# Expert layers with a stationary weight slot instead of turned inner rows

## The chip, the cores and the metric

The kernel runs on one core of a Trainium2 chip. The metric is device time in microseconds (us) of one execution. The engines are TensorE (PE, with its weight loads as PEld), VectorE (DVE), ScalarE (ACT), GpSimd (POOL) and SyncE (SP, which issues most DMAs). They run on their own and meet at semaphores.

## The reference, cut to what matters

A network of four blocks on 2 x 1024 tokens of width 128, all in fp32: a delta-rule attention, a mixture of experts (called f0), a softmax attention, and a second mixture of experts (f1). The change is in f0 and f1.

```
# f0: the two best of 8 experts for each token, hidden width F = 512
h = silu(x @ gate_w[e].T) * (x @ up_w[e].T)       # [tokens, 512]
y = h @ down_w[e].T                               # [tokens, 128]
out += y * gate_of_token
# f1: the best of 8 experts for each token, one down product for all
inter = gelu(x @ W1[e] + b1[e])                   # [tokens, 512]
y = inter @ Wo + bo + x                           # then a layer norm
```

## The kernel before

Tokens are sorted by expert. A tile is 128 rows that share one expert: at most 4096/128 + 7 = 39 tiles in f0 and 2048/128 + 7 = 23 in f1 (`tiles_of`). The layers are written out tile by tile, without a run-time loop; the expert of a tile is known only at run time, so an engine that needs that expert's weights first reads its number from SBUF into a register (`expert_of`, L338) and addresses the weights by the register.

Four functions give the four engines their lists: `experts_pe`, `experts_dve`, `experts_act`, `experts_pool`. In each, a step `s` handles several tiles at different stages (`Lag`): tile s, s-1, s-2, and so on. Nothing reorders the lists. For one tile the stages before are:

- POOL gathers the tile's 128 rows from DRAM into one of 4 slots of `e_x` (L470).
- PE turns them (`turn_x`, L367); DVE copies the turned rows to `e_xt` (L411).
- PE computes the inner product with `e_xt` as stationary operand and the expert's 512 weight columns moving: one matmul of 512 columns (L374), in f0 a second one for the other factor (L394). The result has tokens on partitions.
- f0: ACT takes silu of the first (L448), DVE multiplies by the second (L432). f1: DVE adds the bias of the expert (L418), a tile of [128, 8, 512] which a DMA has repeated over the partitions; ACT takes gelu (L451).
- PE turns the inner rows, four blocks of 128x128 (L389); ACT copies them to `e_ht` (L454). The down product needs the hidden dimension on partitions.
- PE multiplies by the down weights, four matmuls of 128 columns that add up (L383); DVE copies the 128x128 result to `e_y` (L426, below called the y copy); POOL scatters it to DRAM (L475).

An fp32 matmul stands in the trace as two passes, so one inner product is 2 rows, a down product 8, and the four turns of L389 are 4. In f1 DVE also carries four pairs of 128x512 additions (L436) at steps 8, 11, 14 and 17. Ahead of each layer a routing stage on DVE builds the tables; the SP queue meanwhile loads the weights (L639 in f1) and writes the normed rows to DRAM (L564), from which POOL gathers.

Of the kernel before, what the change touches and what calls it, by code (L numbers as in the profile page):

```python
# [11 lines left out]
P = 128  # L12
B, L, D = 2, 1024, 128
# [340 lines left out]
def experts_pe(c, name, top, gated):  # L354
    pe, ps, m, S = c.pe, c.psum, c.mem, c.sem
    n, ident, wup, wdown = tiles_of(top), m["ident"], m["e_up"], m["e_down"]
    xs, xt, h, ht = m["e_x"], m["e_xt"], m["e_h"], m["e_ht"]
    landed = [S(f"{name}_landed{k}") for k in range(SLOTS)]
    turned, copied, up, again = (S(f"{name}_{w}") for w in ("turned", "copied", "up", "again"))
    hidden = S(name + ("_hidden" if gated else "_acted"))  # L360
    hturned, hcopied, down, ready = (S(f"{name}_{w}") for w in ("hturned", "hcopied", "down", "ready"))
    pe.wait_ge(S(name + "_owned"), 1)
    pe.wait_ge(S(name + "_weights"), c.weights)

    def turn_x(a):
        pe.wait_ge(landed[a.slot], 16 * (a.turn + 1))
        pe.transpose(ps[:, 6, 0:P], xs[:, a.slot, :], ident[:]).then_inc(turned, 1)  # L367

    for s in range(n + 3):
        x0, u, g, d = (Lag(s, lag, n) for lag in range(4))  # L370
        if u.there:
            e = expert_of(c, pe, u.t)
            pe.wait_ge(copied, u.t + 1)
            pe.matmul(ps[:, u.pair, :], xt[:, u.pair, :], merged(wup[:, bass.ds(e, 1), 0:F]), start=True, stop=True).then_inc(up, 1)  # L374
        if not gated and x0.there:
            turn_x(x0)
        if d.there:
            ed = bass.ds(expert_of(c, pe, d.t), 1) if gated else slice(0, 1)
            if d.t >= 2:
                pe.wait_ge(ready, d.t - 1)  # L380
            pe.wait_ge(hcopied, d.t + 1)
            for f in range(FC):
                mm = pe.matmul(ps[:, 5 + 2 * d.pair, 0:P], ht[:, f * P:(f + 1) * P], merged(wdown[:, ed, f * P:(f + 1) * P]),  # L383
                               start=f == 0, stop=f == FC - 1)
            mm.then_inc(down, 1)
        if g.there:
            pe.wait_ge(hidden, g.t + 1)
            for f in range(FC):
                mm = pe.transpose(ps[:, 4, f * P:(f + 1) * P], h[:, g.pair, f * P:(f + 1) * P], ident[:])  # L389
            mm.then_inc(hturned, 1)  # L390
        if gated and x0.there:
            turn_x(x0)
        if gated and u.there:
            pe.matmul(ps[:, 2 + u.pair, :], xt[:, u.pair, :], merged(wup[:, bass.ds(e, 1), F:2 * F]),  # L394
                      start=True, stop=True).then_inc(again, 1)
# [5 lines left out]
def experts_dve(c, name, top, gated, x=None):  # L401
# [3 lines left out]
    turned, copied, up, again, acted = (S(f"{name}_{w}") for w in ("turned", "copied", "up", "again", "acted"))  # L405
# [3 lines left out]
    def turn_x(a):  # L409
        dve.wait_ge(turned, a.t + 1)  # L410
        dve.tensor_copy(xt[:, a.pair, :], ps[:, 6, 0:P]).then_inc(copied, 1)  # L411

    for s in range(n + 3):
        x0, u, g, d = (Lag(s, lag, n) for lag in range(4))
        if not gated and u.there:
            e = expert_of(c, dve, u.t)
            dve.wait_ge(up, u.t + 1)
            dve.tensor_tensor(sg[:, u.pair, :], ps[:, u.pair, :], merged(m["e_bias"][:, bass.ds(e, 1), :]), ALU.add).then_inc(hidden, 1)  # L418
        if not gated and x0.there:
            turn_x(x0)  # L420
        if d.there:
# [3 lines left out]
            yp = ps[:, 5 + 2 * d.pair, 0:P]  # L425
            dve.tensor_copy(y[:, d.slot, :], yp).then_inc(ready, 1)  # L426
        if gated and x0.there:
            turn_x(x0)
        if gated and u.there:
            dve.wait_ge(again, u.t + 1)  # L430
            dve.wait_ge(acted, u.t + 1)
            dve.tensor_tensor(h[:, u.pair, :], sg[:, u.pair, :], ps[:, 2 + u.pair, :], ALU.mult).then_inc(hidden, 1)  # L432
# [6 lines left out]
def experts_act(c, name, top, gated):  # L439
    act, ps, m, S = c.act, c.psum, c.mem, c.sem  # L440
    n, sg, h, ht = tiles_of(top), m["e_sg"], m["e_h"], m["e_ht"]
    up, acted, hidden, hturned, hcopied = (S(f"{name}_{w}") for w in ("up", "acted", "hidden", "hturned", "hcopied"))
    act.wait_ge(S(name + "_owned"), 1)
    for s in range(n + 2):
        u, g = Lag(s, 1, n), Lag(s, 2, n)
# [6 lines left out]
        if g.there:  # L452
            act.wait_ge(hturned, g.t + 1)
            act.copy(ht[:], ps[:, 4, :]).then_inc(hcopied, 1)  # L454


def experts_pool(c, name, top, src, dst):
# [21 lines left out]
    for s in range(n + 3):  # L479
        x0, d = Lag(s, 0, n), Lag(s, 3, n)  # L480
# [41 lines left out]
def sorted_memory(c, w, top, up):  # L522
# [3 lines left out]
    for name, shape in (("lo", [P, NT, NE]), ("wide", [P, NT, 32]), ("eq", [P, NT, NE]), ("best", [P, NT]),  # L526
# [6 lines left out]
                        ("e_sg", [P, 2, F]), ("e_h", [P, 2, F]), ("e_ht", [P, F]), ("e_y", [P, SLOTS, D]),  # L533
# [93 lines left out]
def ffn1_memory(c, w):  # L627
# [5 lines left out]
    c.sb("e_bias", [P, NE, F])  # L633


def ffn1_sp(c, w, x, out):
    for name in ("up", "down", "bias"):
        source = w["f1_" + name]
        c.sp.dma_start(c.mem["e_" + name][:], source.partition_broadcast(P) if name == "bias" else source).then_inc(c.sem("f1_weights"), 16)  # L639
# [126 lines left out]
def ffn1_layout(a, out):  # L766
    out["f1_rw"] = np.pad(a["L1_ffn_Wr"].T, ((0, 0), (0, 32 - NE)))
    out["f1_up"] = a["L1_ffn_W1"].transpose(1, 0, 2)
    out["f1_bias"] = a["L1_ffn_b1"]
# [1815 lines left out]
```

## Time and profile before

| | us |
|---|---|
| median of 3 runs | 923.98 (923.12 to 925.49) |
| the profiled execution | 930.92 |
| its span in the profile | 929.6 |
| f0's expert tiles, first turn to the last y copy | 274.7 to 403.2 |
| f1's expert tiles, first turn to the last y copy | 835.7 to 907.6 |

Busy shares over the span: PE 81%, DVE 72%, ACT 55%, POOL 26%. These are means over stages with different limits; the two expert stages are 200 us of the 930 and are read by themselves below. Times in the rows are from the span's start. A row of the timeline merges like instructions that follow each other.

### The profile page before, as it was taken

Reading aid. Unit: us, or ns where it says so; the run is one execution under the profiler, and the core shown is the slowest. Engines: PE = TensorE matmul, PEld = TensorE weight load, DVE = VectorE, ACT = ScalarE, POOL = GpSimd, SP = SyncE. Lnnn points to the kernel's source line nnn. Section 1 sums busy time; section 2 is a strip of 40 time slices with the busy share of each in tenths; the row PEclk is TensorE's granted clock in tenths of the full one; section 3 lists DMA queues with packets and bytes.
Section 4 is the critical chain, followed back from the end, with each engine's and each line's share of the span. In section 5 each row is a group of like instructions: output and inputs, shape, how many; then the busy total and the mean of one; then the engine's idle time right before and its main releaser. Section 6 shows DMA issues by size and latency. Waiting matters only on the chain. (4 is left out here: it accounts for less than half of the span.)

```text
span 929.6 us, 17693 instructions
## 1 busy us (share of the span) xinstructions
PE 756.1 (81%) x6703; PEld 325.6 (35%) x6704; DVE 667.4 (72%) x1316; ACT 511.1 (55%) x1012; POOL 243.9 (26%) x297
## 2 busy tenths in 40 slices
PE   6999978967329999927887999999999999728880
PEld 2343256633216766714111222222222222215660
DVE  7868964477763344338786999999999998753545
ACT  4744413646203333344346888888888889704343
POOL 0130010323055666460651200000010000025653
PEclk9999979988659999977658999999999999958996
DMA  3520010000731111131876030312300000061113
GB/s 94 119 65 2 1 25 5 4 1 0 269 129 38 43 43 43 35 102 52 233 159 194 2 81 2 81 26 58 80 3 2 3 2 12 1 252 44 43 35 96
DMA packets 40618, 57.62 MB, mean 62 GB/s; under 512 B 12424, under 2 KB 27920, under 8 KB 39768
## 3 DMA queue, kind: packets, MB, share of 16 engines
q1 hardware_dynamic: 36568, 48.36, 19.1%
q0 software_dynamic: 3968, 8.13, 3.1%
q8 instruction: 55, 0.90, 0.4%
q14 instruction: 27, 0.22, 0.1%
HBM read 37.54 MB, written 14.75 MB: 56 GB/s over the span
## 5 line engine op out<-in xcount | busy, mean ns | idle before, releaser
L1019 DVE TENSOR_REDUCE arena<-psum 128x1 f32<-128x1024 f32 x256 | 301.0, 1217 | 23.5 <-PE psum L903 20.7
L1158 ACT ACTIVATE arena<-psum 128x512 f32<-128x512 f32 x512 | 265.9, 605 | 53.7 <-PE psum L922 53.6
L903 PE MATMUL psum<-arena 56*128 56x512 bf16 x512 | 181.0, 413 | 10.7 <-DVE arena L1019 9.1
L922 PE MATMUL psum<-arena 59*128 59x512 bf16 x512 | 156.3, 390 | 5.1 <-ACT arena L1158 3.7
L933 PE MATMUL psum<-arena 128*32 128x512 f32 x1024 | 138.4, 612 | 8.7 <-issue 8.7
L922 PEld LDWEIGHTS psum<-arena 59*128 59x128 bf16 x512 | 38.4, 94 | 165.8 <-ACT arena L1158 142.1
L475 POOL DMA_INDIRECT rows_y<-arena x62 | 61.9, 998 | 61.3 <-DVE arena L426 57.9
L383 PEld LDWEIGHTS psum<-arena 128*128 128x128 f32 x496 | 62.4, 191 | 37.9 <-issue 29.5
L383 PE MATMUL psum<-arena 128*128 (+1 forms) x496 | 66.9, 278 | 9.1 <-ACT arena L454 6.0
L374 PE MATMUL psum<-arena 128*128 x124 | 67.2, 625 | 3.5 <-DVE arena L411 2.7
L1227 POOL TENSOR_SCALAR arena<-arena 128x16 f32<-128x16 f32 x16 | 4.1, 254 | 249.5 <-DVE arena L1019 249.4
L470 POOL DMA_INDIRECT arena<-rows_x,arena x62 | 60.1, 969 | 35.4 <-issue 16.1
L903 PEld LDWEIGHTS psum<-arena 56*128 56x128 bf16 x512 | 37.5, 95 | 71.2 <-DVE arena L1019 69.0
L426 DVE COPY arena<-psum 128x128 f32<-128x128 f32 x62 | 18.1, 291 | 58.2 <-issue 36.3
L454 ACT COPY arena<-psum 128x512 f32<-128x512 f32 x62 | 36.2, 584 | 41.3 <-PE psum L389 37.9
L448 ACT ACTIVATE arena<-psum 128x512 f32<-128x512 f32 x39 | 23.3, 597 | 46.9 <-PE psum L374 46.9
L432 DVE TENSOR_TENSOR arena<-arena,psum 128x512 f32<-128x512 f32 x39 | 26.8, 688 | 23.5 <-PE psum L394 22.0
L2242 PE MATMUL psum<-arena 128*32 128x512 f32 x352 | 41.2, 593 | 0.2 <-DMA arena<-arena 0.2
L394 PE MATMUL psum<-arena 128*128 x78 | 40.8, 606 | 0.0
L389 PE MATMUL psum<-ident,arena 128*128 128x128 f32 x248 | 37.7, 275 | 0.0
L933 PEld LDWEIGHTS psum<-arena 128*32 128x32 f32 x1024 | 20.7, 108 | 42.4 <-issue 38.0
L418 DVE TENSOR_TENSOR arena<-psum,arena 128x512 f32<-128x512 f32 x23 | 15.9, 691 | 25.4 <-PE psum L374 19.5
(319 smaller groups left out, 1110.1 us busy)
## 6 DMA issues: line engine op xcount, KB each, us to landing
arena<-scr_k SPq DMA_DIRECT2D x15, 448.0 KB
arena<-scr_q SPq DMA_DIRECT2D x15, 448.0 KB
arena<-in_f_up SPq DMA_DIRECT2D x1, 4096.0 KB
arena<-rows_y SPq DMA_DIRECT2D x12, 256.0 KB, 4.5
scr_q<-arena SPq DMA_DIRECT2D x6, 384.0 KB, 3.7
arena<-in_f_down SPq DMA_DIRECT2D x1, 2048.0 KB
rows_x<-xn SPq DMA_DIRECT2D x2, 1024.0 KB, 16.8
arena<-in_f_up SPq DMA_DIRECT2D x1, 2048.0 KB, 8.4
```

Source lines behind the costliest of these rows:

```text
L374: pe.matmul(ps[:, u.pair, :], xt[:, u.pair, :], merged(wup[:, bass.ds(e, 1), 0:F]), start=True, stop=True).then_inc(up, 1)
L383: mm = pe.matmul(ps[:, 5 + 2 * d.pair, 0:P], ht[:, f * P:(f + 1) * P], merged(wdown[:, ed, f * P:(f + 1) * P]), start=f == 0, stop=f == FC ...
L389: mm = pe.transpose(ps[:, 4, f * P:(f + 1) * P], h[:, g.pair, f * P:(f + 1) * P], ident[:])
L394: pe.matmul(ps[:, 2 + u.pair, :], xt[:, u.pair, :], merged(wup[:, bass.ds(e, 1), F:2 * F]), start=True, stop=True).then_inc(again, 1)
L470: pool.indirect_dma_start(xs[:, t % SLOTS, :], None, src, index).then_inc(landed[t % SLOTS], 16)
L475: pool.indirect_dma_start(dst, index, y[:, d.slot, :], None).then_inc(stored[d.slot], 16)
L903: mm = pe.matmul(ps[:, bank + half, :], q[rows, k, h, (qh * 4 + qt) * P:(qh * 4 + qt + 1) * P], kk[rows, k, h, half * BLK:(half + 1) * BLK ...
L922: pe.matmul(ps[:, score_bank(n), :], kk[0:KA, k, h, kb * P:(kb + 1) * P], q[0:KA, k, h, qh * BLK:(qh + 1) * BLK], start=True, stop=True).t ...
L933: mm = pe.matmul(ps[32 * h:32 * h + 32, 7, :], va[:, kb, (st % NG) * HG + h, :], pt[:, (u % 3) * HG + h, :], start=kb == 0, stop=kb == NTB ...
L1019: dve.tensor_reduce(mx[:, qh, h * 4 + qt:h * 4 + qt + 1], ps[:, bank:bank + 2, :].rearrange("p a b -> p (a b)"), X, ALU.max).then_inc(S("a ...
L1158: act.activation(pt[:, (u % 3) * HG + h, :], ps[:, score_bank(n), :], ACT.Exp, scale=float(HD) ** -0.5).then_inc(S("a1_exp"), 1)
L2242: mm = pe.matmul(ps[32 * h:32 * h + 32, fir_bank(n, i), :], m["a0_wfir"][:, (g0 + g) * H0 + h, :], v4[:, h, b, PAD + t0 - 4 * g:PAD + t0 - ...
```

## The change

The two operands of the inner product change places. The weights become the stationary operand, 128 hidden columns at a time, and the turned tokens `e_xt` the moving one. The result then has the hidden dimension on partitions, as the down product needs it, so `e_ht`, L389 and L454 go. A stationary operand addressed by a register is not used; instead DVE copies the expert's first 512 weight columns to one of two slots `e_w` (new L412), and in f0 ACT copies the other 512 (new L448). Both need the expert's number, so DVE in f0 and ACT in f0 read it now, and DVE in f1 reads it twice. PE reads it once a tile in f0 (for the down weights) and never in f1. The bias of f1 is now one value for each partition and block, [128, 8, 4], loaded by a small DMA and repeated along the free dimension in the addition (new L420). A tile passes through one step fewer: n + 2 steps in place of n + 3.

```
-    for s in range(n + 3):                                            # PE
-        if u.there: e = expert_of(...); wait copied
-            pe.matmul(ps[:, u.pair, :], xt[:, u.pair, :], merged(wup[:, bass.ds(e, 1), 0:F]), ...)
+    def inner(a, half, bank, done):
+        for f in range(FC):
+            at = slice(half * F + f * P, half * F + (f + 1) * P)
+            mm = pe.matmul(ps[:, bank, f * P:(f + 1) * P], w[:, a.pair, at], xt[:, a.pair, :], start=True, stop=True)
+        mm.then_inc(done, 1)
+    for s in range(n + 2):
+        x0, u, d = (Lag(s, lag, n) for lag in range(3))
+        if u.there:
+            pe.wait_ge(copied, u.t + 1)
+            pe.wait_ge(picked, u.t + 1)
+            inner(u, 0, u.pair, up)
+            if gated:
+                pe.wait_ge(picked2, u.t + 1)
+                inner(u, 1, 2 + u.pair, again)
+        if x0.there:   # wait landed, turn the tile's rows
...
-        if g.there:    # wait hidden
-            for f in range(FC):
-                mm = pe.transpose(ps[:, 4, f * P:(f + 1) * P], h[:, g.pair, f * P:(f + 1) * P], ident[:])
...
+        if x0.there:                                                   # DVE
+            e = expert_of(c, dve, x0.t)
+            if x0.t >= 2:
+                dve.wait_ge(up, x0.t - 1)
+            dve.tensor_copy(m["e_w"][:, x0.pair, 0:F], merged(m["e_up"][:, bass.ds(e, 1), 0:F])).then_inc(picked, 1)
+        if u.there and gated:
+            dve.wait_ge(again, u.t + 1)
+            dve.wait_ge(acted, u.t + 1)
+            dve.tensor_tensor(h[:, u.pair, :], sg[:, u.pair, :], ps[:, 2 + u.pair, :], ALU.mult).then_inc(hidden, 1)
...
+        if x0.there and gated:                                         # ACT
+            e = expert_of(c, act, x0.t)
+            if x0.t >= 2:
+                act.wait_ge(again, x0.t - 1)
+            act.copy(m["e_w"][:, x0.pair, F:2 * F], merged(m["e_up"][:, bass.ds(e, 1), F:2 * F])).then_inc(picked2, 1)
...
-        if g.there:
-            act.wait_ge(hturned, g.t + 1)
-            act.copy(ht[:], ps[:, 4, :]).then_inc(hcopied, 1)
...
-    c.sb("e_bias", [P, NE, F])
+    c.sb("e_bias", [P, NE, FC])
```

PE's list in f0 for one tile, before (L338 reads the expert's number, an ISA row forms an address, L374 and L394 are the inner products, L383 the down product, L389 the turns of the inner rows, L367 the turn of the tokens):

```order
L374 ISA [waits f0_copied]
L374 MATMUL psum<-arena 128x512
L338 TENSOR_LOAD arena
L338 ISA x2
L383 ISA [waits f0_hcopied,f0_ready]
L383 MATMUL psum<-arena 128x128
L389 MATMUL psum<-ident,arena 128x128 [waits f0_hidden]
L389 MATMUL psum<-ident,arena 128x128 x3
L367 MATMUL psum<-ident,arena 128x128 [waits f0_landed0]
L394 ISA
L394 MATMUL psum<-arena 128x512
```

and after (L370 is the inner product, its first four for one factor, the next four for the other; L384 the turn of the tokens, L391 the down product):

```order
L370 MATMUL psum<-arena 128x128 [waits f0_picked,f0_copied]
L370 MATMUL psum<-arena 128x128 x3
L370 MATMUL psum<-arena 128x128 [waits f0_picked2]
L370 MATMUL psum<-arena 128x128 x3
L384 MATMUL psum<-ident,arena 128x128 [waits f0_landed0]
L338 TENSOR_LOAD arena
L338 ISA x2
L391 ISA [waits f0_hidden,f0_ready]
L391 MATMUL psum<-arena 128x128
```

The second inner product has moved from behind the turn of the next tile to ahead of it, and both inner products now stand together in front of the turn and the down product.

DVE's list in f0 for two tiles, before (L411 copies the turned tokens, L432 multiplies, L426 is the y copy):

```order
L411 COPY arena<-psum 128x128 [waits f0_turned]
L432 TENSOR_TENSOR arena<-arena,psum 128x512 [waits f0_acted,f0_again]
L426 COPY arena<-psum 128x128 [waits f0_down]
L411 COPY arena<-psum 128x128 [waits f0_turned]
L432 TENSOR_TENSOR arena<-arena,psum 128x512 [waits f0_acted,f0_again]
```

and for one tile and a half after (L412 copies the weights to the slot, L416 multiplies, L424 copies the turned tokens, L429 is the y copy):

```order
L338 TENSOR_LOAD arena
L338 ISA x2
L412 ISA [waits f0_up]
L412 COPY arena<-arena 128x512
L416 TENSOR_TENSOR arena<-arena,psum 128x512 [waits f0_acted,f0_again]
L424 COPY arena<-psum 128x128 [waits f0_turned]
L429 COPY arena<-psum 128x128 [waits f0_down]
L338 TENSOR_LOAD arena
```

The copy of the turned tokens has moved from ahead of the multiplication to behind it.

DVE's list in f1 after, for one tile (L420 adds the bias):

```order
L338 TENSOR_LOAD arena
L338 ISA x2
L412 ISA [waits a0_firm]
L412 COPY arena<-arena 128x512
L338 TENSOR_LOAD arena
L338 ISA x2
L420 ISA [waits a0_firm]
L420 TENSOR_TENSOR arena<-psum,arena 128x512
```

The names of the waits are left over from an earlier use of the same semaphores (here it is `f1_up`). Where one number was read for a tile, two are read now, one ahead of the weight copy and one ahead of the addition.

## Rows read from the trace of the kernel before

**Rows 1.** The page: busy us, share of the span and instructions of each engine.

```profile
PE 756.1 (81%) x6703; PEld 325.6 (35%) x6704; DVE 667.4 (72%) x1316; ACT 511.1 (55%) x1012; POOL 243.9 (26%) x297
```

**Rows 2.** Window in f0: length, busy (count) PE, PEld, DVE, ACT, POOL, clock, DMA.

```profile
300.00:390.00 90.00, 90.00 (x484) 61.78 (x482) 36.39 (x87) 33.69 (x57) 54.74 (x56) 1.00 0.15 42
```

**Rows 3.** Timeline in f0: start, us, engine, line, operation, count, idle before.

```profile
288.46 1.02 PE L374 MATMUL psum<-arena 128*128 x2
288.66 0.69 DVE L432 TENSOR_TENSOR arena<-arena,psum 128x512 f32<-128x512 f32 x1 [0.57 <-PE psum L394]
289.32 1.05 PE L383 MATMUL psum<-arena 128*128 x8
290.21 0.60 PE L389 MATMUL psum<-ident,arena 128*128 128x128 f32 x4
```

**Rows 4.** Timeline: a weight load that waited, once in f0, once in f1.

```profile
279.94 0.69 DVE L432 TENSOR_TENSOR arena<-arena,psum 128x512 f32<-128x512 f32 x1 [1.53 <-issue]
280.68 0.42 PEld L389 LDWEIGHTS psum<-ident,arena 128*128 128x128 f32 x4 [0.86 <-DVE arena L432]
...
868.10 0.97 PEld L383 LDWEIGHTS psum<-arena 128*128 128x128 f32 x8 [1.69 <-issue]
869.10 0.60 PE L389 MATMUL psum<-ident,arena 128*128 128x128 f32 x4
```

**Rows 5.** Timeline of one f1 tile.

```profile
871.25 0.69 DVE L418 TENSOR_TENSOR arena<-psum,arena 128x512 f32<-128x512 f32 x1
871.86 0.28 DVE L411 COPY arena<-psum 128x128 f32<-128x128 f32 x1
872.20 0.29 DVE L426 COPY arena<-psum 128x128 f32<-128x128 f32 x1
873.25 0.27 PE L367 MATMUL psum<-ident,arena 128*128 128x128 f32 x1
873.57 0.69 DVE L418 TENSOR_TENSOR arena<-psum,arena 128x512 f32<-128x512 f32 x1 [1.08 <-PE psum L374]
```

**Rows 6.** Line L338, DVE's queue, 872 to 873.3: ns min/median/max, first and last start.

```profile
L338 DVEq SEQ_ASSERT  x1: 23/23/23, 872.8 to 872.8; - x1
```

**Rows 7.** Groups by shape on DVE: busy us, mean ns, idle before.

```profile
L1636 DVE TENSOR_SCALAR arena<-arena 128x512 f32<-128x512 f32 x8 | 3.5, 483 | 3.3 <-ACT arena L1902 3.3
```

**Rows 8.** POOL in f1: line L475 (as rows 6), then rows of the timeline.

```profile
L475 POOL DMA_INDIRECT rows_y<-arena x23: 967/987/1401, 846.2 to 907.9; - x23
...
861.15 0.69 DVE L436 TENSOR_TENSOR x<-x,arena 128x512 f32<-128x512 f32 x1
861.29 1.40 POOL L475 DMA_INDIRECT rows_y<-arena  x1 [0.30 <-issue]
865.57 0.97 POOL L470 DMA_INDIRECT arena<-rows_x,arena  x1 [0.30 <-issue]
870.35 1.13 POOL L475 DMA_INDIRECT rows_y<-arena  x1 [0.30 <-DVE arena L426]
```

**Rows 9.** Timeline: last inner products of both layers, f0's last y copy, f1's first.

```profile
398.09 1.02 PE L394 MATMUL psum<-arena 128*128 x2
402.91 0.29 DVE L426 COPY arena<-psum 128x128 f32<-128x128 f32 x1 [2.22 <-PE psum L383]
...
836.69 2.07 PE L374 MATMUL psum<-arena 128*128 x2 [0.58 <-DVE arena L411]
...
900.49 1.02 PE L374 MATMUL psum<-arena 128*128 x2
```

**Rows 10.** Timeline: the last table of the routing and the first gather, f0 and f1.

```profile
270.79 0.20 DVE L312 SCALAR_TENSOR_TENSOR arena<-arena 128x40 int32<-128x40 f32 x1
...
271.87 1.19 POOL L470 DMA_INDIRECT arena<-rows_x,arena  x1 [6.50 <-DVE arena L312]
...
831.90 0.18 DVE L312 SCALAR_TENSOR_TENSOR arena<-arena 128x24 int32<-128x24 f32 x1
...
832.88 1.05 POOL L470 DMA_INDIRECT arena<-rows_x,arena  x1 [3.56 <-DMA rows_x<-xn]
```

More of the change, by code:

```diff
@@ L355, in experts_pe @@
     pe, ps, m, S = c.pe, c.psum, c.mem, c.sem
-    n, ident, wup, wdown = tiles_of(top), m["ident"], m["e_up"], m["e_down"]
-    xs, xt, h, ht = m["e_x"], m["e_xt"], m["e_h"], m["e_ht"]
+    n, ident, wdown, w = tiles_of(top), m["ident"], m["e_down"], m["e_w"]
+    xs, xt, h = m["e_x"], m["e_xt"], m["e_h"]
     landed = [S(f"{name}_landed{k}") for k in range(SLOTS)]
-    turned, copied, up, again = (S(f"{name}_{w}") for w in ("turned", "copied", "up", "again"))
+    turned, copied, up, again, picked, picked2 = (S(f"{name}_{w}") for w in ("turned", "copied", "up", "again", "picked", "picked2"))
     hidden = S(name + ("_hidden" if gated else "_acted"))
-    hturned, hcopied, down, ready = (S(f"{name}_{w}") for w in ("hturned", "hcopied", "down", "ready"))
+    down, ready = S(name + "_down"), S(name + "_ready")
     pe.wait_ge(S(name + "_owned"), 1)
     pe.wait_ge(S(name + "_weights"), c.weights)
-    def turn_x(a):
-        pe.wait_ge(landed[a.slot], 16 * (a.turn + 1))
-        pe.transpose(ps[:, 6, 0:P], xs[:, a.slot, :], ident[:]).then_inc(turned, 1)
-    for s in range(n + 3):
-        x0, u, g, d = (Lag(s, lag, n) for lag in range(4))
+    def inner(a, half, bank, done):
[5 more added lines that the diff above has]
+        x0, u, d = (Lag(s, lag, n) for lag in range(3))
         if u.there:
-            e = expert_of(c, pe, u.t)
             pe.wait_ge(copied, u.t + 1)
-            pe.matmul(ps[:, u.pair, :], xt[:, u.pair, :], merged(wup[:, bass.ds(e, 1), 0:F]), start=True, stop=True).then_inc(up, 1)
-        if not gated and x0.there:
-            turn_x(x0)
+            pe.wait_ge(picked, u.t + 1)
[4 more added lines that the diff above has]
+        if x0.there:
+            pe.wait_ge(landed[x0.slot], 16 * (x0.turn + 1))
+            pe.transpose(ps[:, 6, 0:P], xs[:, x0.slot, :], ident[:]).then_inc(turned, 1)
         if d.there:
@@ L380, in experts_pe @@
                 pe.wait_ge(ready, d.t - 1)
[L381 removed]
+            pe.wait_ge(hidden, d.t + 1)
             for f in range(FC):
[L383 removed]
+                mm = pe.matmul(ps[:, 5 + 2 * d.pair, 0:P], h[:, d.pair, f * P:(f + 1) * P], merged(wdown[:, ed, f * P:(f + 1) * P]),
                                start=f == 0, stop=f == FC - 1)
             mm.then_inc(down, 1)
[L386 to L395 removed]
 BIAS_STEPS = {8: 0, 11: 1, 14: 2, 17: 3}
@@ L424, in experts_dve @@
             dve.wait_ge(down, d.t + 1)
[L425 to L432, printed above, removed]
+            dve.tensor_copy(y[:, d.slot, :], ps[:, 5 + 2 * d.pair, 0:P]).then_inc(ready, 1)
         if not gated and s in BIAS_STEPS:
@@ L478, in experts_pool @@
         gather(t)
-    for s in range(n + 3):
-        x0, d = Lag(s, 0, n), Lag(s, 3, n)
+    for s in range(n + 2):
+        x0, d = Lag(s, 0, n), Lag(s, 2, n)
         if top == 1 and x0.there and x0.more:
@@ L638, in ffn1_sp @@
         source = w["f1_" + name]
[L639 removed]
+        c.sp.dma_start(c.mem["e_" + name][:], source).then_inc(c.sem("f1_weights"), 16)
     c.weights = 48
```

34 lines of the change are left out of this document (17 added, 17 removed).

## The prediction, made before the changed kernel ran

> **What bounds the kernel now.** I read the page first: PE is busy 81% of the span [rows 1], but that is a mean over stages, so I went to the windows of the two expert stages. In f0 PE is busy in all 90 of 90 us at full clock, with 484 matmul rows [rows 2]. A tile has 17 of them (1 turn of tokens, 4 for the two inner products, 8 for the down product, 4 turns of inner rows), so 28.5 tiles pass and one takes 3.16 us. The timeline splits it, by starts: an inner product 0.86 (288.46 to 289.32), the down product 0.89 (289.32 to 290.21) [rows 3]. What is left of 3.16, 0.55, is five turns of 0.11. f0 is bound by PE alone: the product that feeds the next step always waits in its queue.
>
> In f1 the sum of the same parts is 0.86 + 0.89 + 5 x 0.11 = 2.30 us, and two additions of the bias stand 2.32 apart in an undisturbed stretch [rows 5]. The whole stage is slower: from the end of the first inner product (836.69 + 2.07 = 838.7) to that of the last (900.49 + 0.86 = 901.35) [rows 9] lie 62.6 us for 22 tiles, 11.6 more than 22 x 2.32 = 51.0. The difference sits in single pauses of 1 to 2 us, as the 1.69 and 1.16 ahead of a down product with "issue" as their cause [rows 4]. I can't name what makes them. I take them as alike in both kernels; that they are not is a rival.
>
> POOL comes next in f1: a gather of 0.97, a scatter of 0.99 and 0.30 of idle ahead of each [rows 8] are 2.56 us a tile, more than PE's 2.32. It holds up nothing only because gathers run four tiles ahead.
>
> **f0, tile by tile.** PE loses four turns (0.44) and pays 2 x 0.89 in place of 2 x 0.86, since eight passes of 128 columns with a new weight each have the shape of the down product. PE's floor is 3 x 0.89 + 0.11 = 2.78 us. I don't take it, because of the order on DVE: the copy of the turned tokens now stands behind the multiplication, which waits for the second inner product, and the next tile's first inner product waits for that copy. This is a closed loop, and it is longer than the floor. From the start of the turn, when the second product has just left PE:
> - to the start of the multiplication 0.20 (288.46 to 288.66) [rows 3];
> - from it to a copy behind it 0.61 (871.25 to 871.86), and the copy 0.28 [rows 5];
> - from the end of a DVE result to PE's weight load 0.05 (279.94 + 0.69 to 280.68) [rows 4];
> - a load that nothing covers: 868.10 to 869.10 is 1.00 where 0.89 is usual, so 0.11 [rows 4];
> - both inner products 1.78.
>
> The sum is 3.03. Meanwhile PE does the turn and the down product (1.00) and idles 0.25. Against 3.16 that is 0.13 x 38 = 4.9 us saved. The bounds: were the wait 0.18 and not 0.05 nothing is saved; at the floor it is 0.38 x 38 = 14.4. I stay with 3.03, as each link has its row.
>
> What was added beside it hides. DVE's weight copy is bounded by 0.48 (a one-input operation of this size [rows 7]) and 0.69 (a two-input one [rows 5]); with a register read (from the copy's start at 872.20 to 872.82, 0.62 [rows 5, 6], and an estimated 0.14 for the address) it ends, behind a y copy that starts 1.2 after the turn, by 1.2 + 0.76 + 0.69 = 2.65, and the multiplication behind it is due at 3.03 + 0.20. ACT trades a copy out of PSUM for one out of SBUF; it is busy 33.69 of 90 us [rows 2]. Without that cover a copy would cost up to 0.69 a tile, 27 us.
>
> A weight load is where a rule of the skill speaks against the change. The down product has the same shape as the new inner product: eight loads and eight passes in 0.89 us, 0.11 a pair [rows 3], so the loads lie behind the passes. The Trainium skill (TensorE: Matmul & The Clock Gate, Part 3, The mechanism) says that a load overlaps matmuls in flight only when its row group differs, and here each load fills all 128 rows. By that rule each load would be laid bare; the trace disagrees.
>
> **f0, the end.** From the end of the last second product (398.09 + 0.86 = 398.95) to the end of the last y copy (402.91 + 0.29) are 4.25 us [rows 9], over multiplication, turns, ACT's copy and down product. After: 0.20 + 0.69 + 0.05 + 0.11 + 0.89 + 0.20 + 0.29 = 2.43. That saves 1.8. f0: -6.7.
>
> **f1.** Two loops run beside each other. Through PE: 0.32 from the turn's start to the addition (873.25 to 873.57 [rows 5]; its address costs more than in f0), 0.61, 0.28, 0.05, 0.11, 0.89, sum 2.26. Through DVE alone: y copy, read of the number and address 0.76, weight copy, a second read 0.76 (issued as soon as the weight copy is), addition, 0.61 to the tokens' copy, and 0.20 to the y copy (0.34 where it waits [rows 5]): 2.33. So the pace stays at 2.32 and PE's four turns bring nothing. The four pairs of additions L436 (0.60 from one start to the next) hold DVE 1.2 each, of which the register reads cover all but some 0.35: +1.4. The end, from the last product to the end of the last scatter, is 907.9 + 0.97 - 901.35 = 7.5 us now [rows 8, 9]; after, 0.32 + 0.69 + 0.05 + 0.70 for gelu (an estimate, by the addition) + 0.05 + 0.11 + 0.89 + 0.20 + 0.29 + 0.28 + 0.97 = 4.55, so -3.0. By PE and DVE, f1 gains 1.6.
>
> POOL takes part of it. The slowest scatter, 1.40 in place of 0.99, ran beside an addition with two SBUF inputs on DVE, and the one of 1.13 likewise [rows 8]: beside such work POOL loses 0.14 to 0.41. The weight copy now runs every tile and POOL has no idle time to lose. Without pauses, f1 now ends at 838.7 + 51.0 + 7.5 = 897.2, and after, by PE, at 895.6. POOL has 38 operations left when it starts its first scatter (15 gathers, 23 scatters), 38 x 1.28 = 48.6; it starts some 1.8 earlier than 846.2 [rows 8], so it ends at 893.0 + 20 x (0.14 to 0.41) = 895.8 to 901.2. I take 0.18, by the smaller of the two stretched rows: 896.6, so f1 gains 0.6, with bounds of -1.6 and +4.0.
>
> The Trainium skill (GPSIMD Engine Reference, section 8, Key points) says that POOL shares its SBUF interfaces with VectorE and that two-port modes and two SBUF inputs contend. The stretched rows agree for two inputs; no row shows the copy's own mode.
>
> The bias now moves 16 KB and not 2 MB, and the first gather of f1 is shown as waiting for the rows' DMA [rows 10]. That looks like a gain and is none: the last table was ready at 832.08, and f0's gather, which waited for that table alone, began 0.88 after it (270.99 to 271.87), which here gives 832.96, where the gather began at 832.88. Bounds 0 and -0.5; I take 0.
>
> **Sum.** -6.7 - 0.6 = -7.3 us. The profiled execution took 930.92 (span 929.6), so 923.6 in a profile. The median of the runs is 6.9 below the profiled one; with the same distance the forecast is 923.98 - 7.3 = 916.7.
>
> **Rivals.**
> - No gain in f0's loop. Its links are single readings, and 0.13 more (a wait of 0.18) brings it to 3.16. Only the ends and f1 are left: -1.8 - 0.6 = -2.4, 921.6. For it: the margin is 4% of a tile. Against: each link is a row. 19%.
> - POOL binds f1. At 0.41 a tile f1 loses 4.0: -6.7 + 4.0 = -2.7, 921.3. In f0 POOL would need 2.56 + 0.41 = 2.97, still under 3.03. 12%.
> - DVE binds f1, the slower side. If a register read begins only when DVE has finished what is ahead of it, y copy 0.29 + 0.76 + 0.48 + 0.76 + 0.61 + 0.20 = 3.10 a tile: +0.78 x 22 = 17.2, with the end -3.0 and f0 -6.7 it is +7.5, 931.5. It decides from a pace of 2.32 + 9.7 / 22 = 2.76. Against: the reads finish 0.62 after the y copy's start while that copy lasts 0.29 [rows 5, 6], and one cannot tell from this pair whether the read waited. 17%.
> - The pauses in f1 go away. PE's list gets shorter and loses its register reads there: -7.3 - 11.6, 905.1. For it: they have no named cause and f0 has none. Against: the same. 9%.
> - The weight loads are laid bare: 0.19 more for each of 8 passes, 101 products, +150 us. 1%.
>
> The forecast itself has 42%, with a range of 912 to 921. Faster or slower is told from no change at 0.3%, 2.8 us, so at 921.2. The forecast, the fourth rival and half of the first two fall on the faster side, together 0.66, rounded to 0.65; the other half is no change, with a little of the slower rival at a lower price: 0.17; slower 0.18. The range of 907 to 927 leaves out the far ends of the third and fourth.
>
> **What would show it.** In f0, PE with a gap of about 0.25 us ahead of each first inner product, released by DVE's copy of the tokens, and a pace of 3.03; a pace of 2.8 or 3.2 proves the loop wrong. From f0's last second product to the last y copy 2.4. In f1, a pace near 2.3 between pauses, POOL without idle time, scatters of 1.1 to 1.4; a pace of 3.1 with DVE idle behind register reads is the slower rival. The first gather of f1 still about 0.9 behind L312. The forecast falls if the pauses differ in number.

## The result, and the profile after

The changed kernel takes 916.13 us (median, 914.98 to 918.17, four runs), the kernel before 923.55 (921.95 to 925.49, four runs): ratio 0.9929, interval 0.9908 to 0.995, which is 7.4 us faster (4.6 to 8.5 by the interval). The forecast was 916.7. The profiled executions differ by more, 929.6 to 916.8 in span, and most of this part is about where those 12.8 us and the 7.4 agree and where they don't. One result ahead of all: on another chip the same change made the kernel 6.6 us slower, by pauses of a kind that the trace of before shows in f1.

f0 first, the timeline of the changed kernel (start, duration, engine, line, operation, shapes, idle time before it and what released it). One tile runs from L416 to L416:

```profile
288.09 0.14 PEld L384 LDWEIGHTS psum<-ident,arena 128*128 128x128 f32 x1
288.20 0.27 PE L384 MATMUL psum<-ident,arena 128*128 128x128 f32 x1
...
288.31 1.06 PE L391 MATMUL psum<-arena 128*128 x8
288.40 0.69 DVE L416 TENSOR_TENSOR arena<-arena,psum 128x512 f32<-128x512 f32 x1 [0.84 <-PE psum L370]
...
289.01 0.28 DVE L424 COPY arena<-psum 128x128 f32<-128x128 f32 x1
289.34 1.86 PEld L370 LDWEIGHTS psum<-arena 128*128 128x128 f32 x16 [0.17 <-DVE arena L424]
...
290.17 0.43 DVE L412 COPY arena<-arena 128x512 f32 x1 [0.48 <-issue]
...
291.12 0.14 PEld L384 LDWEIGHTS psum<-ident,arena 128*128 128x128 f32 x1
291.23 0.27 PE L384 MATMUL psum<-ident,arena 128*128 128x128 f32 x1
...
291.43 0.69 DVE L416 TENSOR_TENSOR arena<-arena,psum 128x512 f32<-128x512 f32 x1 [0.83 <-PE psum L370]
```

These lines answer to [rows 3]. Read them as a ring: the turn's pass starts at 288.20, the multiplication 0.20 later, the copy of the tokens 0.61 after that, it ends at 289.29, PE's load follows 0.05 later at 289.34, and the next turn's pass stands at 291.23, 1.89 on: 3.03 in all. The only idle time in PE's records is the 0.17 that L370's load waits for L424; against the floor of 2.78 the wait costs 0.25.

The windows (busy time and number of instructions per engine, granted clock, DMA share, GB/s) show why the busy share would have misled:

```profile
300.00:390.00 90.00, 90.00 (x744) 84.91 (x743) 47.77 (x119) 36.12 (x60) 56.80 (x59) 1.00 0.16 45
845.00:885.00 40.00, 35.47 (x281) 32.26 (x279) 30.04 (x73) 10.07 (x16) 30.86 (x31) 1.00 0.18 50
```

PE reads 90.00 of 90, as before [rows 2], though it waits in every tile: the modelled ends of the passes cover a gap of 0.2 us. What tells is the number of loads, 743 in place of 482.

f1 is bound by VectorE in more than half of its tiles now, and by PE in the others. POOL's lines show that it isn't POOL:

```profile
857.60 0.68 DVE L420 TENSOR_TENSOR arena<-psum,arena 128x512 f32<-128x512 f32 x1
...
858.40 0.27 DVE L429 COPY arena<-psum 128x128 f32<-128x128 f32 x1
...
859.84 0.69 DVE L420 TENSOR_TENSOR arena<-psum,arena 128x512 f32<-128x512 f32 x1 [0.54 <-PE psum L370]
...
860.45 0.28 DVE L424 COPY arena<-psum 128x128 f32<-128x128 f32 x1
...
860.79 0.29 DVE L429 COPY arena<-psum 128x128 f32<-128x128 f32 x1
861.41 0.97 POOL L470 DMA_INDIRECT arena<-rows_x,arena  x1 [0.30 <-issue]
861.57 0.43 DVE L412 COPY arena<-arena 128x512 f32 x1 [0.48 <-issue]
...
862.33 0.69 DVE L420 TENSOR_TENSOR arena<-psum,arena 128x512 f32<-128x512 f32 x1 [0.34 <-PE psum L370]
...
863.34 0.68 DVE L433 TENSOR_TENSOR xn<-xn,arena 128x512 f32<-128x512 f32 x1
863.94 0.68 DVE L433 TENSOR_TENSOR x<-x,arena 128x512 f32<-128x512 f32 x1
863.97 1.49 POOL L470 DMA_INDIRECT arena<-rows_x,arena  x1 [0.30 <-issue]
```

From L420 at 859.84 to L420 at 862.33 are 2.49 us, all of it VectorE's own list: 0.61 to the tokens' copy, 0.34 to y, 0.78 to the weight copy, 0.76 to the next addition. The 0.48 ahead of L412, put down to "issue", is the read of the tile's expert number. The interval ahead of it (857.60 to 859.84) is 2.24, the loop through PE. The 22 intervals of the stage have a mean of 2.52 (836.11 to 891.55). The first two are 3.18 and 3.53, and PE's granted clock was 0.50 there, 1.2 GHz:

```profile
836.00:842.00 6.00, 5.11 (x24) 4.95 (x24) 2.61 (x7) 2.54 (x3) 2.60 (x4) 0.50 0.13 37
```

The other 20 have a mean of 2.44: eight lie at 2.24 to 2.33, where the addition starts 0.32 to 0.39 behind PE's turn, as with an idle VectorE, and twelve at 2.42 to 2.73, where it starts 0.49 to 0.79 behind, held by VectorE's own list. The gather beside the weight copy (861.41) takes 0.97 as ever, the one beside the two-input additions 1.49.

The ends, from the same timeline, answer to [rows 9]:

```profile
397.60 0.69 DVE L416 TENSOR_TENSOR arena<-arena,psum 128x512 f32<-128x512 f32 x1 [1.67 <-PE psum L370]
...
398.54 0.97 PEld L391 LDWEIGHTS psum<-arena 128*128 128x128 f32 x8 [0.28 <-issue]
...
399.81 0.29 DVE L429 COPY arena<-psum 128x128 f32<-128x128 f32 x1 [0.96 <-PE psum L391]
...
891.55 0.69 DVE L420 TENSOR_TENSOR arena<-psum,arena 128x512 f32<-128x512 f32 x1 [1.17 <-PE psum L370]
...
894.85 0.96 POOL L475 DMA_INDIRECT rows_y<-arena  x1 [0.93 <-DVE arena L429]
```

From first turn to last y copy f0 takes 122.4 us where it took 128.5: 6.1 less. From first turn to the end of the last scatter f1 takes 62.8 where it took 73.2, 10.4 less; the stretches ahead of f0, between the layers and behind f1, which the change doesn't touch, are 3.8 longer in sum. The 10.4 hold the pauses of 1 to 2 us that the profiled f1 of before had. Its time, 930.92, is none of the four timed ones and lies 5.4 above the slowest of them, while every other profiled execution here is among its kernel's timed runs or, for the repeat of the kernel before, within the range of those beside it. So the timed runs of before had fewer pauses than the profiled one, or that one ran on another chip; on which it ran isn't on record.

### The profile page after: what moved, and what is told of

Read it like the earlier page. It is cut to its first block and busy times, and to the rows that moved or that the text cites. A ratio compares the mean times of both kernels' runs of the same rounds, so it can differ in the third digit from the quotient of the medians.

```text
span 916.8 us, 18626 instructions
## 1 busy us (share of the span) xinstructions
PE 747.2 (82%) x7061; PEld 364.4 (40%) x7062; DVE 689.2 (75%) x1378; ACT 499.5 (54%) x989; POOL 245.0 (27%) x297
## 5 line engine op out<-in xcount | busy, mean ns | idle before, releaser
L370 PE MATMUL psum<-arena 128*128 128x128 f32 x808 | 110.9, 290 | 7.9 <-DVE arena L424 7.2
L370 PEld LDWEIGHTS psum<-arena 128*128 128x128 f32 x808 | 99.0, 198 | 19.4 <-DVE arena L424 19.4
L475 POOL DMA_INDIRECT rows_y<-arena x62 | 62.1, 1001 | 47.7 <-DVE arena L429 43.1
L470 POOL DMA_INDIRECT arena<-rows_x,arena x62 | 60.9, 982 | 31.6 <-issue 16.8
L391 PE MATMUL psum<-arena 128*128 (+1 forms) x496 | 66.5, 278 | 0.9 <-ACT arena L454 0.8
L391 PEld LDWEIGHTS psum<-arena 128*128 128x128 f32 x496 | 61.1, 194 | 1.2 <-DVE arena L429 0.9
L451 ACT ACTIVATE arena<-psum 128x512 f32<-128x512 f32 x39 | 23.3, 597 | 59.6 <-PE psum L370 59.6
L416 DVE TENSOR_TENSOR arena<-arena,psum 128x512 f32<-128x512 f32 x39 | 26.8, 686 | 33.4 <-PE psum L370 33.4
L412 DVE COPY arena<-arena 128x512 f32 x62 | 27.3, 440 | 26.6 <-issue 26.1
L448 ACT COPY arena<-arena 128x512 f32 x39 | 24.1, 619 | 34.8 <-DVE arena L303 19.5
L454 ACT ACTIVATE arena<-arena 128x512 f32<-128x512 f32 x23 | 14.5, 630 | 40.2 <-DVE arena L420 40.2
L1982 ACT ACTIVATE arena<-psum 128x64 f32<-128x64 f32 x32 | 7.2, 224 | 41.8 <-PE psum L2264 41.7
```

The lines of the kernel that those rows point to most:

```text
L370: mm = pe.matmul(ps[:, bank, f * P:(f + 1) * P], w[:, a.pair, at], xt[:, a.pair, :], start=True, stop=True)
L391: mm = pe.matmul(ps[:, 5 + 2 * d.pair, 0:P], h[:, d.pair, f * P:(f + 1) * P], merged(wdown[:, ed, f * P:(f + 1) * P]), start=f == 0, stop= ...
L412: dve.tensor_copy(m["e_w"][:, x0.pair, 0:F], merged(m["e_up"][:, bass.ds(e, 1), 0:F])).then_inc(picked, 1)
L470: pool.indirect_dma_start(xs[:, t % SLOTS, :], None, src, index).then_inc(landed[t % SLOTS], 16)
L475: pool.indirect_dma_start(dst, index, y[:, d.slot, :], None).then_inc(stored[d.slot], 16)
```

## The experiments

Twelve runs were made, on four chips, here called A to D; each chip was used for one stretch of time only, so what is put down to a chip below could also belong to the moment. Whether the chip of the forecast is one of them isn't on record. The kernel before was timed on each beside them. "Interval" is the time from one DVE operation behind the inner product (L416 or its like in f0, L420 in f1) to the next; a pause is an interval more than 0.7 above the median. In f1 the median itself varies (2.25 to 2.79), and most counts take in one or both of the first two intervals (3.2 to 3.6 us, the slow start). On chip B these are all that is counted, but for one of 3.34 in the version with both edits. Of pauses past the start, the kernels on chips A and C have four to six in f1.

| kernel | chip | us | before | ratio | f0 interval, pauses | f1 interval, pauses |
|---|---|---|---|---|---|---|
| f0 only | A | 944.82 | 934.86 | 1.010 | 3.47, 11 | 2.89, 7 |
| f1 only | A | 932.31 | 934.86 | 0.996 | 3.14, 0 | 2.91, 5 |
| before | A | 936.66 | 934.86 | (one run) | 3.14, 0 | 2.96, 7 |
| one more load | A | 939.51 | 934.86 | 1.0055 | 3.41, 10 | 2.90, 6 |
| changed | B | 914.98 | 922.00 | 0.992 | 3.03, 0 | 2.55, 1 |
| early copy in f0 | B | 904.69 | 922.00 | 0.980 | 2.77, 0 | 2.53, 1 |
| f1's copy on ACT | B | 912.65 | 922.00 | 0.989 | 3.03, 0 | 2.40, 2 |
| both | B | 900.19 | 922.00 | 0.975 | 2.77, 0 | 2.31, 1 |
| f0 only | C | 941.61 | 932.93 | 1.009 | 3.40, 9 | 2.99, 4 |
| changed | C | 939.55 | 932.93 | 1.007 | 3.43, 10 | 2.94, 5 |
| double copy in f0 | C | 937.66 | 932.93 | 1.0045 | 3.41, 10 | 2.93, 6 |
| both | D | 901.20 | 922.45 | 0.978 | 2.77, 0 | 2.30, 0 |

**One half at a time, chip A.** One layer got the new functions, the other kept the old ones, POOL's list included.

```
 f0 only:  ffn0_*: experts_pe / _dve / _act        ffn1_*: experts_pe_old / _dve_old / _act_old
 f1 only:  ffn0_*: experts_pe_old / _dve_old / ..  ffn1_*: experts_pe / _dve / _act
```

> f0 as changed, f1 as before. Theory (the loop of f0 is 3.03 us a tile, its end 1.8 us shorter, and f1's share in the runs is small): 6.1 to 6.7 us faster than the kernel before, pace in f0 3.03, f1 with pauses of 1 to 2 us in the profile as in the kernel before. Rival (the 10 us by which f1 is shorter in the profile of the changed kernel are also in the timed runs): f0 alone brings only what is left of 7.4, near 0.

Measured: 944.82 us (944.04 to 946.87), ratio 1.010 (1.0076 to 1.0124). A miss, by 16 us and in sign. Its intervals run 3.0, 3.0, 4.5, 3.0, 3.0, 4.8 and so on: the forecast pace, with about 1.5 us put in at every third tile.

> f1 as changed, f0 as before. Theory: 0.6 to 1.6 us faster than the kernel before, at most 2, with f1's pace 2.45 us a tile in the profile, bound by DVE, and no pauses. Rival (the pauses are in timed runs too and the change removes them): about 7 to 10 us faster.

Measured: 932.31 (930.85 to 934.44), ratio 0.9961 (0.9942 to 0.998), 2.5 us less (1.9 to 5.4 by the interval), for 0.6 to 1.6 expected. f1 gains a little, and it has pauses, where none were expected.

> The kernel before, unchanged, profiled once more. Theory (the pauses in f1 belong to that kernel's f1 when it is profiled): they come back, f1 from the first turn to the last y copy takes 70 to 73 us, and the profiled run is 5 to 7 us above the median. Rival (they were an accident of one execution): f1 takes about 61 us, and no pause over 1 us is seen there.

Measured: 936.66, in one run. The old f1 pauses on this chip (2.96 a tile where 2.33 is the median), the old f0 never. The pauses came back, with f1 at 74.4 us, but the profiled run is 1.8 above the median of the timed ones, not 5 to 7: here they are in the timed runs too. The old f1's 22 intervals are 65.2 us, 12.8 more than 22 x 2.32 and the 1.3 of its slow start; the kernel before takes 12.9 more on chip A than on chip B. By that estimate the old f1 has next to no pauses on chip B, where it was never profiled.

**One more load ahead of the rows, chip A.** A second copy of f1's 2 MB weights is loaded on the SP queue ahead of the write of the rows.

```
     c.sp.dma_start(c.mem["e_up"][:], w["f1_up"]) ...
+    c.sp.dma_start(c.mem["e_more"][:], w["f1_up"]).then_inc(c.sem("f1_weights"), 16)
```

> The changed kernel with one more load of 2 MB (f1's inner weights once more, to an unused place) ahead of the DMA that writes f1's rows. Theory (the smaller bias brings nothing, because the routing tables are as late as the rows): the rows land some 7 us later than in the changed kernel, which is near the tables' time, so the first gather moves by 0 to 2 us and the time by 0 to 2 us. Rival (the 2 MB saved on the bias are part of the gain): the first gather moves by 5 us or more and the time with it.

Measured: 939.51 (936.58 to 943.43). The first gather of f1 in the changed kernel, then in this one:

```profile
830.18 1.20 POOL L470 DMA_INDIRECT arena<-rows_x,arena  x1 [3.56 <-DVE arena L312]
```

```profile
843.36 1.06 POOL L470 DMA_INDIRECT arena<-rows_x,arena  x1 [4.76 <-DMA rows_x<-xn]
```

The releaser turns from the tables (L312) to the rows' DMA, and the gather starts 2.18 after L312's start (841.18) in place of 0.98 (829.20). So with one more load the rows are late by 1.2 us; in the changed kernel the tables are last. In the kernel before it was 0.98 as well (831.90 to 832.88 [rows 10]), though that row named the DMA. The smaller bias load thus bought nothing, as the sum had it. What the added load costs in time isn't shown, as the changed kernel wasn't timed on chip A.

**The changed kernel again, and three edits of VectorE's order, chip B.**

> The changed kernel with nothing altered, beside the kernel before on the same chip, timed in five rounds. It is here because the kernel with only f0 changed came out about 10 us slower than before, with a pause of about 1.5 us at every third tile of f0 (mean interval 3.47 instead of 3.03) that the changed kernel did not have in its own profile. Theory A, the pauses belong to the place and moment the program runs in, not to its instructions: this run shows them too where the others of its call do, and then it is 0 to 5 us slower than before; where none of them has pauses it is 7 us faster (ratio 0.993). Theory B, they hang on the code's layout (the parts unchanged in the f0-only kernel make it differ): here there are none in f0, interval 3.03, ratio 0.993 wherever it runs.

Measured: 914.98 (913.47 to 918.71, seven runs), ratio 0.9924 (0.9893 to 0.9955), all 38 intervals of f0 at 3.03. Both theories allow this.

The next kernel copies the turned tokens ahead of the multiplication in f0:

```
+        if x0.there and gated:
+            dve.wait_ge(turned, x0.t + 1)
+            dve.tensor_copy(xt[:, x0.pair, :], ps[:, 6, 0:P]).then_inc(copied, 1)
         if u.there and gated:
             ... dve.tensor_tensor(h ...)
-        if x0.there:
+        if x0.there and not gated:
```

> The changed kernel, but in f0 VectorE copies the turned tokens ahead of the h multiplication instead of behind it. Theory (the prediction's closed loop): PE idles in f0 only because the copy of the turned tokens stands behind the multiplication; ahead of it the multiplication's 0.69 us and the semaphores lie beside PE's work, and f0's interval falls from 3.03 to the PE floor of 2.78, so 38 x 0.25 = 9.6 us less than the changed kernel of the same call. Rival: VectorE's own order (weight copy, copy, multiplication, y copy) then holds the weight copy of the next tile back and the interval stays near 3.03: no change.

Measured: 904.69 (903.35 to 907.41), 10.3 less than the changed kernel on this chip. Its timeline:

```profile
301.28 1.06 PE L391 MATMUL psum<-arena 128*128 x8
...
301.48 0.29 DVE L415 COPY arena<-psum 128x128 f32<-128x128 f32 x1 [0.62 <-PE psum L384]
...
301.69 0.68 DVE L419 TENSOR_TENSOR arena<-arena,psum 128x512 f32<-128x512 f32 x1
302.07 1.87 PEld L370 LDWEIGHTS psum<-arena 128*128 128x128 f32 x16
...
303.85 0.14 PEld L384 LDWEIGHTS psum<-ident,arena 128*128 128x128 f32 x1
```

L370's loads have no wait any more, the interval is 2.79 in nearly all tiles (mean 2.77), and VectorE waits for PE instead: the floor of 2.78 that the prediction worked out and didn't take. Only the place of one copy has changed, so the closed loop is shown to be what held f0 at 3.03.

f1's weight copy on ScalarE:

```
-        if x0.there:                        # experts_dve
+        if x0.there and gated:
+        if x0.there and not gated:          # experts_act
+            act.copy(m["e_w"][:, x0.pair, 0:F], merged(m["e_up"][:, bass.ds(e, 1), 0:F])).then_inc(picked, 1)
```

> The changed kernel, but in f1 the copy of an expert's inner weights is made by ScalarE instead of VectorE. In the profile of the changed kernel f1 runs at a steady 2.24 to 2.73 us a tile, with VectorE as its bound. Theory: without the 0.43 us copy and its register read f1 falls to the PE floor of about 2.26 at every tile, and the bias additions hide: 23 x 0.2 = 4 to 6 us less than the changed kernel of the same call. Rival (PE or the gathers bound f1 already): no more than 1 us.

Measured: 912.65 (912.21 to 913.02), 2.3 less than the changed kernel, below the 4 to 6 expected but well over the rival's 1.

```profile
855.64 0.69 DVE L420 TENSOR_TENSOR arena<-psum,arena 128x512 f32<-128x512 f32 x1 [1.15 <-PE psum L370]
...
856.36 0.63 ACT L459 ACTIVATE arena<-arena 128x512 f32<-128x512 f32 x1 [0.99 <-DVE arena L420]
...
856.58 1.16 PE L370 MATMUL psum<-arena 128*128 128x128 f32 x8
...
857.90 0.69 DVE L420 TENSOR_TENSOR arena<-psum,arena 128x512 f32<-128x512 f32 x1 [1.02 <-PE psum L370]
```

The interval is 2.26 here, the prediction's loop through PE to the hundredth, and VectorE waits 1 us a tile. The mean of the stage is 2.40, from 2.55: 22 x 0.15 = 3.4 in the profile.

> The changed kernel with the copy of the turned tokens ahead of the other VectorE work in both layers, and f1's weight copy on ScalarE. If the two gains are independent it is the sum of the other two kernels of this call: 12 to 16 us less than the changed kernel of this call. If the pauses follow the load on PE (a busier PE has none, as the kernel before in f0), its f0 has no pauses even where the changed kernel's has them.

Measured: 900.19 (898.02 to 902.35), ratio 0.9751 (0.9709 to 0.9793), 14.8 less than the changed kernel: inside the 12 to 16, with the two gains of 10.3 and 2.3 and some 2 more from f1's early copy (mean interval 2.31).

**Chip or code? Chip C.** Chip A had shown pauses, chip B none, and no kernel had run on both except the one before.

For f0 only:

> The kernel with f0 changed and f1 left as before, once more: in its first run it was 10 us slower than before, with 11 pauses of about 1.5 us in f0 that the changed kernel, with the same f0 code, doesn't have in its own two profiles (interval 3.03 throughout). Theory A, the pauses belong to the chip: where the changed kernel of this call has none, this one has none, f0's interval is 3.03, and it is 6.1 to 6.7 us faster than before; where this one has them, the changed kernel has them too. Theory B, they belong to the code (f1's old form): here they are again and the changed kernel of this call has none, 10 us slower than before.

For the changed kernel:

> The changed kernel again, as the partner of the f0-only kernel and of the doubled copy on the same chip. Theory A (pauses belong to the chip) and no pauses: 7 us faster than before, f0's interval 3.03; with pauses in f0: about equal to before, +-3 us. Theory B (they belong to the code): 3.03 and 7 us faster, whatever the f0-only kernel does.

Measured: f0 only 941.61 (940.61 to 945.43), ratio 1.0092 (1.0065 to 1.0119); the changed kernel, word for word, 939.55 (937.03 to 943.57), ratio 1.0068 (1.0047 to 1.009), 6.6 us slower than before, where about equal (+-3) was expected with pauses. Both have the pauses in f0. Theory B has fallen: the same instructions run at 3.03 throughout on chip B and at a mean of 3.43 on chip C. The windows of the changed kernel on chip C:

```profile
300.00:390.00 90.00, 78.59 (x649) 74.08 (x648) 39.83 (x103) 31.62 (x52) 50.96 (x52) 1.00 0.12 39
```

and one pause in its timeline, with the undisturbed tile ahead of it:

```profile
323.99 1.86 PEld L370 LDWEIGHTS psum<-arena 128*128 128x128 f32 x16 [0.17 <-issue]
...
325.18 0.60 ACT L451 ACTIVATE arena<-psum 128x512 f32<-128x512 f32 x1 [1.43 <-issue]
...
326.08 0.69 DVE L416 TENSOR_TENSOR arena<-arena,psum 128x512 f32<-128x512 f32 x1 [0.63 <-PE psum L370]
...
327.02 1.86 PEld L370 LDWEIGHTS psum<-arena 128*128 128x128 f32 x16 [0.17 <-issue]
...
327.92 0.43 DVE L412 COPY arena<-arena 128x512 f32 x1 [0.48 <-issue]
...
329.01 0.97 POOL L470 DMA_INDIRECT arena<-rows_x,arena  x1 [0.30 <-issue]
...
329.13 0.60 ACT L451 ACTIVATE arena<-psum 128x512 f32<-128x512 f32 x1 [2.34 <-PE psum L370]
330.58 0.69 DVE L416 TENSOR_TENSOR arena<-arena,psum 128x512 f32<-128x512 f32 x1 [2.23 <-PE psum L370]
```

From L370's first load to the multiplication that needs its last pass are 2.09 us, then 3.56. The loads and passes stand in the record as evenly as ever; those who wait for PE's semaphores (L451 by 0.9, L416 by 1.5) start late, and those who don't (DVE's L412, POOL's L470) run on. The granted clock is 1.00 in the window of 300 to 390 on both chips. So it is PE's results, or the signal that they are there, that come late, and PE's own records don't show it; the two aren't told apart here. The idle time turns up one step later, ahead of PE's next inner product: the window reads 78.59 of 90.

**A second weight copy a tile, chip C.**

```
+            if gated:
+                dve.tensor_copy(m["e_more"][:, x0.pair, :], merged(m["e_up"][:, bass.ds(e, 1), 0:464]))
```

> The changed kernel, and in f0 VectorE makes a second copy of 464 of the 512 columns of the inner weights a tile, into a place nobody reads. The prediction put f0's weight copy at nothing, since it ends by 2.65 of 3.03 us behind a copy of y. A second one of 0.39 to 0.44 us ends at about 3.05 to 3.1 and lets the multiplication of the next tile, due at 3.23, start on time. Theory (copy hidden, closed loop sets the pace): interval stays 3.03, 0 to +1 us. Rival (VectorE's work or its port, shared with GpSimd, is near the bound): +0.1 to +0.43 us a tile, 4 to 16 us.

Measured: 937.66 (935.35 to 941.29), beside 939.55 for the changed kernel on this chip; the ranges overlap.

```profile
290.81 1.05 POOL L477 DMA_INDIRECT rows_y<-arena  x1 [1.03 <-DVE arena L431]
...
291.35 0.40 DVE L414 COPY arena<-arena 128x464 f32 x1
...
299.57 0.69 DVE L418 TENSOR_TENSOR arena<-arena,psum 128x512 f32<-128x512 f32 x1 [1.24 <-PE psum L370]
...
301.34 0.98 POOL L477 DMA_INDIRECT rows_y<-arena  x1 [1.18 <-DVE arena L431]
301.55 0.43 DVE L412 COPY arena<-arena 128x512 f32 x1 [0.49 <-issue]
...
301.89 0.63 DVE L414 COPY arena<-arena 128x464 f32 x1
...
302.60 0.69 DVE L418 TENSOR_TENSOR arena<-arena,psum 128x512 f32<-128x512 f32 x1
```

The interval between pauses stays 3.03 but for three tiles of 3.25 to 3.43: the extra 0.63 ends at 302.52, just ahead of the multiplication. The weight copy in f0 is hidden, with more than its own length to spare, and POOL binds nothing. The rows show, all the same, that copy and scatter get in each other's way. At the same place in its tile the copy took 0.40 once, with the scatter at 1.05, and 0.63 once, with the scatter at 0.98. So it is in the whole stage: eleven of the 39 copies took 0.39 or 0.40 beside a scatter stretched to 1.04 to 1.06, and fourteen took 0.62 to 0.65 beside one of 0.97 to 0.99.

**Gap or rate? Chip D.** The version with both edits keeps PE busy as the old f0 does, and loads more weights per us than any other.

> The kernel with the tokens' copy first in VectorE's order in both layers and f1's weight copy on ScalarE, once more, in five rounds. Where f0's intervals were 3.03 it was 21.8 us faster than before (0.975). On two other chips the changed kernel had 10 pauses of about 1.5 us in f0, the old f0 none. The old f0 keeps PE busy all the time and passes 17 rows in 3.16 us; the changed f0 leaves PE 0.25 us of idle a tile and passes 25 rows in 3.03 us; this one keeps PE busy and passes 25 rows in 2.78 us. On a chip with pauses: theory G (a gap of PE brings the pause): none in f0, interval 2.77, and 15 to 22 us faster than before. Theory R (the rate of rows and weight loads brings it): 10 or more pauses in f0, mean interval 3.1 to 3.3, and 0 to 10 us faster than before. On a chip without pauses in any kernel: 0.975 again, and the question stays open.

Measured: 901.20 (898.54 to 905.62), ratio 0.9778 (0.9744 to 0.9812), no pauses. But chip D, where before takes 922.45, is by that time of the kind of chip B, so this doesn't tell a gap in PE's work from a rate of loads as what brings the pauses. What it does show is that the faster version holds its gain on a second chip: 21 us.

## Why the prediction was right, point by point

**f0's pace: right.** 3.03 forecast, 3.033 measured, link by link (0.20, 0.61, 0.28, 0.05, 1.89), and the early copy took the loop away and found the floor. The first rival (no gain in the loop) and the one of the laid-bare weight loads are out: L370's 16 loads take 1.86 us, 0.12 each.

**f0's end: nearly.** From the last second product to the last y copy 2.43 were forecast. Counting 0.20 ahead of the last multiplication, it is 0.20 + (400.10 - 397.60) = 2.70. Of the 0.27 above, 0.20 is the down product, whose loads start 0.94 behind the multiplication's start where 0.74 was forecast, after 0.28 of "issue". The 38 intervals are 3.9 less in sum (119.2 to 115.3) and not 4.9, mainly because the old f0's first and last took 2.41 and 3.05, not 3.16. With the end 1.55 less and the start 0.6 less, f0 gained 6.1 for 6.7.

**f1's pace: mis-sized.** It was put at 2.32 for all 22 intervals, with 1.4 in all for the additions, 52.4; measured are 55.4. Of the 3.0 between, 2.1 are the first two intervals, which run at the granted clock of 0.50; the old f1 has such a start too (3.27 and 2.68, 1.3 above 2.32), and the prediction left it out on both sides. The other 0.9 is of the size of one mis-sized link, from the tokens' copy to y, taken at 0.20, the value for an operation that doesn't wait for data. It is 0.20 in twelve of the other 20 tiles and 0.26 to 0.34 in eight, 0.9 us in sum; in the tile shown above it is 0.34, as in [rows 5] where it does wait. The register reads were right (0.78 and 0.76 for 0.76), and the slower rival (reads that begin only when VectorE has finished, 3.10 a tile) is out: 2.24 to 2.73 in all but the first tiles. Moving the copy to ScalarE gave the 2.26 of the other loop in most tiles, which shows that VectorE was the bound of those above it.

**f1 and POOL: the mechanism doesn't bind.** 0.18 was added to each gather and scatter; the mean of the 46 in f1 went from 0.99 to 1.015, 0.02. Those over 1.1 us are seven in place of four, and the long ones (1.49, 1.25) stand beside or just behind L433, the pairs with two SBUF inputs. Beside the one-input weight copy most gathers and scatters take 0.97 to 1.00. The contention is there but falls on either side: three of the 23 weight copies in f1 took 0.57 to 0.67 and not 0.43, as the second copy in f0 took 0.63. The Trainium skill (GPSIMD Engine Reference, section 8, Key points) names two inputs in SBUF and two-port modes as what contends; the first is what the 1.49 shows. That a one-input copy contends is shown by the doubled copy in f0; whether in such a mode no row tells.

**f1's end: right.** 0.32 + (895.81 - 891.55) = 4.58, forecast 4.55.

**The sum: right in part by luck.** From the end of the first inner product to the last scatter the forecast for f1 was 896.6 - 838.7 = 57.9; measured are 895.81 - (836.11 - 0.32) = 60.0. Of the 2.1 above, the slow start is as much; the mis-sized link and the POOL term that wasn't there about cancel. Without its pauses, but with its own slow start, the old f1 took 897.2 - 838.7 + 1.3 = 59.8 on the same measure. So f1 by itself is even, where 0.6 less was forecast, and the traces account for 6.1 - 0.2 = 5.9 of the timed gain. That lies inside the interval of 4.6 to 8.5: the timed runs need no change in the pauses, and can't exclude one of some us. A forecast of 7.3 that meets 7.4 is thus closer than its terms deserve. In the two profiles the pauses of f1 did go, as the fourth rival had it: of the 62.8 us from the old f1's first addition to its last some 10 are pauses, and the new one has none past its start. If the profiled run of before met another chip, that is a difference of chips and not of kernels; no run on record settles it.

**The pauses: the assumption that failed elsewhere.** "I take them as alike in both kernels" did no harm in the timed runs of the forecast. On chips A and C it is false, and it costs more than the whole gain. There f0, which had none in the old form (profiled on chip A), gets ten or so in the new one: 38 x (3.43 - 3.14) = +11.0, less 1.6 at its end, less 2.1 from f1 (from the timed runs, 939.55 against 941.61 on chip C) is +7.3, and 6.6 were measured. The same sum closes for f0 only on chip A: 38 x (3.47 - 3.14) - 1.6 = +10.9, measured +10.0.

## What to carry to other kernels

When PE and VectorE hand work to and fro within a tile, write the ring of waits out from timeline rows before looking at busy shares: here it gave the pace to a hundredth, and it named the one copy whose place was worth 10 us. Count each link by what it waits for (0.34 after a wait, 0.20 without), and count the start of a stage by itself when the granted clock is low there. And a pause in the trace that has no cause is a term of its own: ask whether the change moves work into the regime where it occurs, and time the change on more than one chip before its sign is believed. A profiled run that lies outside the timed ones is a warning of the same kind.

## What the runs showed of the hardware that was not expected

- **Pauses of about 1.5 us behind PE, on some chips.** In the new f0 most come 10 to 14 us apart, and they last 0.7 to 1.9 us; in f1 5 to 15 us lie between them. By weight loads per us: the old f0 (482 in 90 us, 5.4) had none in the three profiles there are, the one of before and two on chip A; the old f1 (15 in 2.33 us between pauses, 6.4) had three to six past its start in four profiles, none of them on B or D; the new f1 (17 in 2.26 to 2.44 us, 7.0 to 7.5) had four to six on A and C and none on B; the new f0 (8.3) had none on chip B and nine to eleven on A and C; the version with both edits (9.0 in f0) had none on B and D. On chips A and C the kernel before takes 933 to 935 us, on B and D 922. A rate of loads or rows above some bound, or gaps in PE's work, fit these numbers alike; the version that would tell them apart met no chip with pauses. The 16 KB instruction fetches don't line up with them: on chip C they are some 15 us apart in f0, the pauses 10 to 14. The cause stays open.
- **A full busy share of PE can hide a short gap.** PE read 90.00 of 90 with 0.17 us of wait in the records of each tile, 0.25 against the floor. A pause isn't in the record where it happens: the passes stand at their usual spacing while those who wait for them are 1.5 us late, and the share falls (78.59 of 90) by the wait behind it. The number of passes in a window, or the intervals of the engine that waits, tell the truth.
- **A copy on VectorE and a scatter of POOL can hold each other up.** Of the 39 copies of 128x464 in f0, 14 took 0.62 to 0.65 us, all of them beside a scatter of 0.97 to 0.99 that had started 0.55 to 0.56 ahead; the one with no POOL operation beside it took 0.38, and eleven with a scatter of 1.04 to 1.06 took 0.39 or 0.40. Which of the two pays turned on some 0.01 us of start. That it is their access to SBUF is an inference; no run took POOL's work away.
